# Idle products on TensorE ahead of three steps, each in the bank of the step that follows

## Chip, cores and metric

The kernel runs on one core of one Trainium2 chip. The metric is the device time of one execution in microseconds (us), as the median of several runs. The profile is of one further execution.

## The reference

Two layers on x of 4 sequences x 512 tokens x 256 features, in float32. What matters here:

```python
xn = layernorm(x)
x = x + L0_attn(xn) + L0_ffn(xn)     # elu feature maps, cumsum over tokens; top-32 of 512 genes
xn = layernorm(x)
x = x + L1_attn(xn) + L1_ffn(xn)

def L1_attn(x):
    q, k, v = split(rms(x) @ w_qkv.T)         # 256 each
    q, k = rms(q), rms(k)
    w = exp(k)
    y = sigmoid(q) * (cumsum(w * v) / (cumsum(w) + 1e-6))
    u, g = split(y @ w_swiglu.T)              # 1024 each
    return x + u * silu(g) @ w_out.T

def L1_ffn(x):                                # 16 experts, each token goes to 2
    y = sum over the two experts e of p_e * (swiglu(x @ w_gate_up[e]) @ w_down[e])
    return y + swiglu(x @ shared_gate_up) @ shared_down
```

## The kernel before

Each engine has its own order of steps, written out by hand as a list of calls in its block of the program. Engines meet only through semaphores. A step is a small function with the sequence b (0 to 3) and mostly a half or chunk, and on TensorE the PSUM bank that it writes: `dgate(0, 2, 5)` is the gate half of chunk 2 of sequence 0's gated products, into bank 5.

Ahead of about 340 us runs the front: for each sequence the first layer (turn1, logits, kproj, vproj, qproj, emturn, express, ffn, oproj), then the second layer's attention (turnr, turn2, qproj2, meanq, gates, kproj2, meank, vproj2) and the eleven chunks of dense gated products (dgate, dup, ddown). Behind it 47 tiles of 128 rows go through the routed experts (xturn, xup, hturn, xdown), mixed with the last sequence's chunks.

The eight banks are handed out by hand. `Banks.take` (and TensorE's `take`) waits until what last read the bank has given it back, and notes which semaphore and value will give it back next. Banks 6 and 7 accumulate ddown's products over a whole sequence. Banks 0 to 5 serve the other steps.

The steps around the change:

- `qproj2`, `kproj2`, `vproj2` (b, j): six products of 128x512 in fp32r each, from w_qkv1's high and low parts and FE, FF. They wait for rlow (DVE, L1006), the step's operands. The bank of qproj2 is given back by qhat (DVE, L1011), that of kproj2 by khat (L1018), that of vproj2 by wvtimes (L1023).
- `meanq` and `meank` (L395, L400): the mean of the squares as a float32 product. They wait for a fold on POOL, qfold (L1321) or kfold (L1325), which waits for the squares on ACT (L708). Behind meank: krms on ACT (L721, L723), then khat on DVE.
- `gates` (b): the router's logits, read by gatea (DVE) and so given back.
- `dgate`, `dup` (b, k): six products of 128x512 in fp32r each. All products made with the helper `products` have line 280.
- `awake(n)` (L292 for its product): n float32 products of a constant tile, 128x256, without a reader, into bank 6. It stands at eight places ahead of 73 us in the order.

In the order of TensorE the three places are: behind turnr(1, 0), turnr(1, 1) and ahead of dgate(0, 2); behind kproj2(1, 1) and ahead of meank(1); behind dup(1, 8) and ahead of kproj2(3, 0). The last step in the bank named by each new call: vproj2(0, 0) in bank 5, gates(1) in bank 2, qproj2(3, 0) in bank 5.

Of the kernel before, what the change touches and what calls it, by code (L numbers as in the profile page):

```python
# [83 lines left out]
def build(nc, x, vec, cst, wqkv0, wo0, wc, genes, wdu, wqkv1, wsg, wout, gate, sgu, sdn, gu, dn, part_d, out):  # L84
    with ExitStack() as ctx:
# [129 lines left out]
        banks = Banks([ctx.enter_context(nc.psum_tensor(f"bank{n}", [P, 512], F32)) for n in range(8)])  # L215
        bank_of = {}

        def ps(*key):
            return banks.t[bank_of[key]]
# [31 lines left out]
        def low_made(b, k):  # L251

            return s["rlp" if SPLIT[b] else "rl"], CHUNKS * sum(z == SPLIT[b] for z in SPLIT[:b]) + k + 1
# [11 lines left out]
        def chunk_of(k):  # L265

            if k < 3:
                return sgv, k * P, 352 + k * P, "sdn", min(P, 352 - k * P), k
            n = (k - 3) % 2 * P
            return [w[:, (k - 3) // 2] for w in wgv], D + n, n, "wout", P, k - 3  # L270
# [4 lines left out]
        def tensor(e):  # L275
            q = Queue(e)

            def products(o, terms):
                for n, (a, b) in enumerate(terms):
                    mm = e.matmul(o, a, b, start=n == 0, stop=n == len(terms) - 1)  # L280
                return mm

            def take(key, n, sem, value):
                bank_of[key] = n
                return banks.take(q, n, sem, value)

            def awake(n):

                q.wait_ge(s["wdr"], 1)
                o = banks.t[6]  # L290
                for _ in range(n):
                    e.matmul(o[:, 0:D].rearrange("p (k t) -> p k t", t=P), still[:, :], still[:, None, :].broadcast_to([P, 2, P]), start=True, stop=True)  # L292

            def turn1(b, h, n):
# [63 lines left out]
            def turnr(b, c, n):  # L358
                o = take(("tr", b, c), n, s["rlo"], 2 * b + c + 1)
                q.wait_ge(s["xr"], 4 * b + 4)  # L360
                for i in range(NT):
                    mm = e.transpose(o[:, i * P:(i + 1) * P], FDr[b % 2][:, i, c * P:(c + 1) * P], ident)
                mm.then_inc(s["tr"], 1)

            def turn2(b, c, n):
                o = take(("t2", b, c), n, s["x2"], 2 * b + c + 1)
                q.wait_ge(s["xn2"], 4 * b + 4)
                for i in range(NT):
                    mm = e.transpose(o[:, i * P:(i + 1) * P], FGw[b % 2][:, i, c * P:(c + 1) * P], ident)
                mm.then_inc(s["t2"], 1)  # L370

            def project2(b, j, n, first, sem, back, key):
                q.wait_ge(s["pl"], 1)
                o = take((key, b, j), n, back, 2 * b + j + 1)
                q.wait_ge(s["rlo"], 2 * b + 2)
                terms = []
                for c in range(2):
                    a, al = (w[:, c, (first + j) * P:(first + j + 1) * P] for w in qkv1)
                    h, l = FEr[b % 2][:, c, :], FFr[b % 2][:, c, :]
                    terms += [(a, h), (al, h), (a, l)]  # L380
                products(o[:, :], terms).then_inc(sem, 1)

            def qproj2(b, j, n):
                project2(b, j, n, 0, s["q2"], s["hq"], "q2")

            def kproj2(b, j, n):
                project2(b, j, n, 2, s["k2"], s["hk"], "k2")

            def vproj2(b, j, n):
                project2(b, j, n, 4, s["v3"], s["wv"], "v3")  # L390

            def meanq(b, n):
                o = take(("mq", b), n, s["rq"], 2 * b + 1)
                q.wait_ge(s["sqf"], b + 1)
                e.matmul(o[:, :], mean, FC[b % 2][:, 0, :], start=True, stop=True).then_inc(s["mq"], 1)  # L395

            def meank(b, n):
                o = take(("mk", b), n, s["rk"], 2 * b + 1)
                q.wait_ge(s["skf"], b + 1)
                e.matmul(o[:, :], mean, FC[b % 2][:, 0, :], start=True, stop=True).then_inc(s["mk"], 1)  # L400

            def gates(b, n):
                q.wait_ge(d["gate"], loaded["gate"])
                o = take(("gm", b), n, s["gt"], 7 * b + 2)
                q.wait_ge(s["x2"], 2 * b + 2)
                for i in range(NT):
                    mm = products(o[:, i * E:(i + 1) * E], [(FA[b % 2][:, c, i * P:(i + 1) * P], gtv[:, c, :]) for c in range(2)])
                mm.then_inc(s["gm"], 1)

            def hidden(b, k, n, first, sem, back, value, key):  # L410
                w, _, _, _, m, _ = chunk_of(k)
                h, l, made = (XH, HXr, s["xl"]) if k < 3 else (YH, HYr, s["yl"])
                q.wait_ge(s["pl"], HIDDEN[k])
                o = take((key, b, k), n, back, value)
                q.wait_ge(made, 2 * b + 2)
                terms = []
                for c in range(2):
                    a, al = (z[:, c, first:first + m] for z in w)
                    terms += [(a, h[:, c, :]), (al, h[:, c, :]), (a, l[:, c, :])]
                products(o[0:m, :], terms).then_inc(sem, 1)  # L420

            def dgate(b, k, n):
                back, value = (s["tg"], CHUNKS * b + k + 1) if DIRECT[b] else (s["g2"], CHUNKS * sum(not z for z in DIRECT[:b]) + k + 1)
                hidden(b, k, n, chunk_of(k)[1], s["dg"], back, value, "dg")

            def dup(b, k, n):
                hidden(b, k, n, chunk_of(k)[2], s["du"], s["dh"], CHUNKS * b + k + 1, "du")

            def ddown(b, k, n0, n1):
                _, _, _, name, m, r = chunk_of(k)  # L430
                oh, ol = pairs[name]
                if k == 0:
                    take(("acc", b, 0), n0, s["od"], 2 * b + 1)
                    take(("acc", b, 1), n1, s["od"], 2 * b + 2)
                c = CHUNKS * b + k
                q.wait_ge(s["pl"], DOWN[k])
                q.wait_ge(*low_made(b, k))
                for i in range(NT):
                    o = ps("acc", b, i // 2)[:, (i % 2) * D:(i % 2 + 1) * D]
                    h0, h1 = (h[0:m, 0, i * P:(i + 1) * P] for h in (HQ[c % 2], HSr[c % 2]))  # L440
                    for z, (a, w) in enumerate(((h0, oh), (h0, ol), (h1, oh))):
                        mm = e.matmul(o, a, w[0:m, r, :], start=k == 0 and i % 2 == 0 and z == 0, stop=False, skip_group_check=True)  # L442
                mm.then_inc(s["dw"], 1)
# [7 lines left out]
            def routed(g, *n):  # L451
                if g == 0:
                    take(("tab",), *n, s["rt"], 21)
                o = ps("tab")
                q.wait_ge(s["oh"], g + 1)

                for k in range(4):
                    mm = e.matmul(o[:, 0:3 * TW], r_bt[g % 2][:, k * P:(k + 1) * P], r_at[g % 2][:, 3 * TW * k:3 * TW * (k + 1)],
                                  start=g == 0 and k == 0, stop=False, skip_group_check=True)
                mm.then_inc(s["rtm"], 1)  # L460
# [54 lines left out]
            turnr(0, 1, 1); awake(2); emturn(1, 1, 5); turn2(0, 1, 1); qproj2(0, 0, 3); qproj2(0, 1, 5); qproj(1, 1, 0); emturn(1, 2, 1); express(1, 1)  # L515
            meanq(0, 2); gates(0, 0); emturn(1, 3, 1); express(1, 2); express(1, 3); kproj2(0, 0, 2); ffn(1, 0, 3); kproj2(0, 1, 1); ffn(1, 1, 5)
            ffn(1, 2, 0); dgate(0, 0, 4); ffn(1, 3, 3); dup(0, 0, 5); meank(0, 0); oproj(1, 0, 3); oproj(1, 1, 4); vproj2(0, 0, 5); vproj2(0, 1, 0)
            dgate(0, 1, 2); ddown(0, 0, 6, 7); dup(0, 1, 1); turnr(1, 0, 3); turnr(1, 1, 4); dgate(0, 2, 5); qproj2(1, 0, 3); qproj2(1, 1, 0)
            turn2(1, 0, 4); turn2(1, 1, 2); dup(0, 2, 1); meanq(1, 4); gates(1, 2); kproj2(1, 0, 5); kproj2(1, 1, 1); meank(1, 2); vproj2(1, 0, 4)
            ddown(0, 1, 6, 7); vproj2(1, 1, 3); dgate(0, 3, 0); turn1(2, 0, 2); dup(0, 3, 5); logits(2, 0, 1); ddown(0, 2, 6, 7); logits(2, 1, 4)  # L520
            turn1(2, 1, 3); dgate(0, 4, 2); kproj(2, 0, 3); logits(2, 2, 0); logits(2, 3, 1); dup(0, 4, 4); dgate(0, 5, 5); ddown(0, 3, 6, 7)
            emturn(2, 0, 3); dup(0, 5, 2); dgate(0, 6, 4); kproj(2, 1, 0); dup(0, 6, 5); express(2, 0, 3); ddown(0, 4, 6, 7); vproj(2, 0, 2)
# [9 lines left out]
            dup(1, 3, 4); ddown(1, 2, 6, 7); dgate(1, 4, 1); vproj2(2, 1, 2); dup(1, 4, 3); turn2(3, 0, 5); turn2(3, 1, 4); dgate(1, 5, 0)  # L532
            ddown(1, 3, 6, 7); gates(3, 1); dup(1, 5, 2); turnr(3, 0, 5); turnr(3, 1, 3); ddown(1, 4, 6, 7); dgate(1, 6, 4); dup(1, 6, 0); route1(1)
            dgate(1, 7, 2); qproj2(3, 0, 5); dup(1, 7, 4); qproj2(3, 1, 3); ddown(1, 5, 6, 7); ddown(1, 6, 6, 7); meanq(3, 0); dgate(1, 8, 0)
            dup(1, 8, 1); kproj2(3, 0, 5); kproj2(3, 1, 3); dgate(1, 9, 2); ddown(1, 7, 6, 7); dup(1, 9, 4); routed(0, 0); dgate(1, 10, 1)
            ddown(1, 8, 6, 7); dup(1, 10, 2); meank(3, 4); dgate(2, 0, 1); ddown(1, 9, 6, 7); routed(1); dup(2, 0, 2); vproj2(3, 0, 4); routed(2)
            dgate(2, 1, 1); ddown(1, 10, 6, 7); vproj2(3, 1, 5); dup(2, 1, 3); dgate(2, 2, 2); dup(2, 2, 4); ddown(2, 0, 6, 7); dgate(2, 3, 1)
            ddown(2, 1, 6, 7); dup(2, 3, 3); dgate(2, 4, 2); routed(3); ddown(2, 2, 6, 7); dup(2, 4, 4); dgate(2, 5, 1); dup(2, 5, 5); ddown(2, 3, 6, 7)
# [1034 lines left out]
```

## Time and profile before

| | us |
|---|---|
| median of 3 runs | 539.07 |
| lowest and highest | 535.23 and 539.32 |
| the profiled execution | 531.5 |
| its span | 529.7 |

The span is the time from the first to the last record of the profiled execution. The execution's own time has 1.8 us around it. It is shorter than all three other runs. Times in the rows are counted from the start of the span. PE is TensorE's products, PEld its weight loads. One float32 product of `awake` is two MATMUL records, and so is one of `meank`. The granted clock 1.00 is 2.4 GHz, 0.50 is 1.2 GHz.

### The profile page before, as it was taken

To read this page: it belongs to the slowest core of one execution; us is meant where nothing else is said; L and a number is where in the kernel's file an instruction comes from. 1 tells how busy PE (TensorE), PEld (TensorE's weight loads), DVE (VectorE), ACT (ScalarE), POOL (GpSimd) and SP (SyncE) were. 2 spreads that over 40 slices of the span, in tenths; PEclk is the share of its full clock that TensorE was granted. 3 is DMA by queue.
4 is the path that set the end of the run, shared out by engine and by line. 5 is a ranking of instruction groups with operands and counts; after the bars stand their busy time and mean duration, and the time that the engine had idled before them with its cause. 6 is when DMAs were issued, how large, how long until landed. Compare 5 with 4: busy or idle time off the path is not lost.

```text
span 529.7 us, 7444 instructions
## 1 busy us (share of the span) xinstructions
PE 507.5 (96%) x2488; PEld 384.8 (73%) x2488; DVE 354.0 (67%) x735; ACT 296.0 (56%) x577; POOL 272.7 (51%) x207
## 2 busy tenths in 40 slices
PE   7989999988999999999997999999999999999995
PEld 5565577766577766877885888887777777777684
DVE  4999995786998998847899895743232323323347
ACT  3788798785767758767653636225343343424321
POOL 0475648383472373383256346464576576666510
PEclk9999999998999999999999999999999999999999
DMA  8900031026020001037001850583322232223267
GB/s 271 372 6 1 1 124 37 0 100 220 1 80 40 1 1 41 1 129 243 1 1 44 292 179 14 187 232 98 108 91 89 71 100 83 97 80 89 71 242 265
DMA packets 19813, 54.32 MB, mean 103 GB/s; under 512 B 3312, under 2 KB 5792, under 8 KB 19776
## 3 DMA queue, kind: packets, MB, share of 16 engines
q1 hardware_dynamic: 15264, 41.52, 22.7%
q0 software_dynamic: 4512, 12.33, 7.7%
q8 instruction: 21, 0.34, 0.3%
q14 instruction: 16, 0.13, 0.1%
HBM read 36.14 MB, written 17.74 MB: 102 GB/s over the span
## 4 chain that ended last, share of the span: by engine, by line
PE 74%; DVE 15%; DMA 4%; issue 3%; ACT 2%; POOL 1%; SPq 1%; DVEq 0%; POOLq 0%; ACTq 0%
PE bank L280 52%; PE bank L442 9%; PE bank L355 3%; PE bank L474 2%; PE bank L501 2%; DMA fa<-in_x 2%; DMA ga<-y_rows 2%; DVE tk L972 1%; DVE m L970 1%; PE bank L328 1%; DVE fe L1029 1%; PE bank L400 1%; PE bank L292 1%; DVE tk L978 1%; DVE rw L1235 1%
## 5 line engine op out<-in xcount | busy, mean ns | idle before, releaser
L1214 DVE TENSOR_TENSOR m_h<-m_h,bank 128x176 f32<-128x176 f32 x47 | 15.8, 337 | 82.9 <-ACT m_h L789 82.9
L280 PE MATMUL bank<-mw,m_xt 128*128 x188 | 66.4, 476 | 0.2
L1362 POOL DMA_INDIRECT y_rows<-m_y,dest x47 | 46.9, 997 | 30.7 <-DVE m_y L1221 20.9
L1356 POOL DMA_INDIRECT xg<-xn_rows,tab x47 | 45.5, 969 | 28.0 <-PE bank L474 19.3
L280 PE MATMUL bank<-yhr,wsg_h 128*128 128x512 f32 x128 | 56.0, 437 | 0.8 <-ACT fc L721 0.8
L280 PE MATMUL bank<-hyr,wsg_h 128*128 128x512 f32 x128 | 50.1, 392 | 0.0
L280 PE MATMUL bank<-yhr,wsg_l 128*128 128x512 f32 x128 | 50.1, 391 | 0.0
L280 PE MATMUL bank<-mw,m_ht 88*128 x188 | 48.3, 379 | 0.0
L280 PE MATMUL bank<-fe,w_qkv 128*128 128x512 f32 x96 | 44.5, 594 | 0.6 <-ACT fe L622 0.6
L1347 POOL TENSOR_TENSOR hs0r<-hs,hq0r 128x512 fp32r<-128x512 f32 (+1 forms) x17 | 23.4, 1374 | 39.8 <-ACT hq0r L776 39.8
L280 PEld LDWEIGHTS bank<-mw,m_ht 88*128 88x128 f32 x188 | 35.2, 189 | 11.1 <-issue 0.4
L280 PEld LDWEIGHTS bank<-mw,m_xt 128*128 128x128 f32 x188 | 32.0, 189 | 14.9 <-issue 2.3
L789 ACT ACTIVATE m_h<-bank 128x176 f32<-128x176 f32 x47 | 14.9, 317 | 46.5 <-PE bank L280 46.5
L1098 DVE SCALAR_TENSOR_TENSOR hs<-hs,bank 128x512 f32<-128x512 f32 (+1 forms) x44 | 29.9, 680 | 14.7 <-PE bank L280 7.9
L1301 POOL TENSOR_TENSOR tk<-tk 128x512 f32<-128x512 f32 x16 | 21.3, 1334 | 27.9 <-ACT tk L680 27.8
L1347 POOL TENSOR_TENSOR hs1r<-hs,hq1r 128x512 fp32r<-128x512 f32 (+1 forms) x16 | 21.1, 1321 | 28.0 <-ACT hq1r L776 28.0
L782 ACT ACTIVATE m_xt<-bank 128x256 f32<-128x256 f32 x47 | 17.9, 381 | 29.9 <-PE bank L474 29.9
L572 ACT ACT_TABLE_LOAD x23 | 29.5, 1283 | 6.7 <-PE bank L442 5.6
L1088 DVE SCALAR_TENSOR_TENSOR hs<-hs,bank 128x512 f32<-128x512 f32 (+1 forms) x33 | 22.4, 680 | 15.4 <-ACT hs L771 15.4
L280 PEld LDWEIGHTS bank<-fe,w_qkv 128*128 128x128 f32 x96 | 17.5, 190 | 18.2 <-issue 16.3
L280 PE MATMUL bank<-w_wc,fe 128*128 128x512 f32 x64 | 29.9, 594 | 0.9 <-DVE w_wc L859 0.9
L280 PEld LDWEIGHTS bank<-yhr,wsg_h 128*128 128x128 f32 x128 | 24.1, 189 | 7.5 <-issue 1.7
(241 smaller groups left out, 1419.7 us busy)
## 6 DMA issues: line engine op xcount, KB each, us to landing
mw<-in_gu SPq DMA_DIRECT2D x16, 352.0 KB
ga<-y_rows SPq DMA_DIRECT2D x8, 512.0 KB, 8.1
mw<-in_dn SPq DMA_DIRECT2D x16, 176.0 KB
wsg_w<-in_wsg SPq DMA_DIRECT2D x4, 512.0 KB, 14.8
spilled_r<-fb SPq DMA_DIRECT2D x4, 512.0 KB, 2.8
spilled_x<-fa SPq DMA_DIRECT2D x4, 512.0 KB, 4.0
xn_rows<-fg SPq DMA_DIRECT2D x4, 512.0 KB, 3.6
hx<-spilled_x SPq DMA_DIRECT2D x4, 512.0 KB, 3.7
```

Source lines behind the costliest of these rows:

```text
L280: mm = e.matmul(o, a, b, start=n == 0, stop=n == len(terms) - 1)
L355: mm = e.matmul(o[:, i * D:(i + 1) * D], FF[b % 2][:, c, t:t + P], wov[:, c, :], start=False, stop=i + c == 2, skip_group_check=True)
L442: mm = e.matmul(o, a, w[0:m, r, :], start=k == 0 and i % 2 == 0 and z == 0, stop=False, skip_group_check=True)
L572: e.preload_act_table_set(name)
L782: e.activation(m_xt[j % 2][:, :], ps("jx", j)[:, 0:D], ACT.Copy).then_inc(s["jxc"], 1)
L1088: e.scalar_tensor_tensor(h, h, 1.0, ps("dg", b, k)[0:m, :], ALU.add, ALU.mult).then_inc(s["g2"], 1)
L1098: e.scalar_tensor_tensor(h[0:m, 1, :], h[0:m, 0, :], 1.0 if DIRECT[b] else 0.5, ps("du", b, k)[0:m, :], ALU.mult, ALU.mult).then_inc(s["dh ...
L1214: e.tensor_tensor(m_h[j % 3][:, :], m_h[j % 3][:, :], ps("ju", j)[:, 176:352], ALU.mult).then_inc(s["jh"], 1)
L1301: e.tensor_tensor(em, em, w, ALU.subtract).then_inc(s["tc"], 1)
L1347: e.tensor_tensor(HSr[c % 2][0:m, 0, :], HS[c % 2][0:m, 1, :], HQ[c % 2][0:m, 0, :].bitcast(F32), ALU.subtract).then_inc(s["rlp"], 1)
L1356: e.indirect_dma_start(out=xg[j % 3][:, :], out_offset=None, in_=xn_d, in_offset=bass.IndirectOffsetOnAxis(ap=tab[:, j:j + 1], axis=0)).th ...
L1362: e.indirect_dma_start(out=y_d, out_offset=bass.IndirectOffsetOnAxis(ap=dest[:, j:j + 1], axis=0), in_=m_y[j % 3][:, :], in_offset=None).t ...
```

## The change

`awake` takes the number of products and a bank, bank 6 if none is given. It waits until that bank has been given back, without taking it: the step behind it takes the bank as before. The eight calls from before stay in bank 6. There is one difference for them in principle, a wait on bank 6's giver, but they all stand ahead of the first step that takes bank 6, so there is nothing to wait for. Three calls are added. No other step moves, on any engine.

```diff
-            def awake(n):
+            def awake(k, n=6):
 
                 q.wait_ge(s["wdr"], 1)
-                o = banks.t[6]
-                for _ in range(n):
+                if banks.back[n]:
+                    q.wait_ge(*banks.back[n])
+                o = banks.t[n]
+                for _ in range(k):
                     e.matmul(o[:, 0:D].rearrange("p (k t) -> p k t", t=P), still[:, :], still[:, None, :].broadcast_to([P, 2, P]), start=True, stop=True)
...
-            ... turnr(1, 0, 3); turnr(1, 1, 4); dgate(0, 2, 5); ...
+            ... turnr(1, 0, 3); turnr(1, 1, 4); awake(3, 5); dgate(0, 2, 5); ...
-            ... kproj2(1, 0, 5); kproj2(1, 1, 1); meank(1, 2); ...
+            ... kproj2(1, 0, 5); kproj2(1, 1, 1); awake(6, 2); meank(1, 2); ...
-            dup(1, 8, 1); kproj2(3, 0, 5); kproj2(3, 1, 3); ...
+            dup(1, 8, 1); awake(8, 5); kproj2(3, 0, 5); kproj2(3, 1, 3); ...
```

## Rows read from the trace of the kernel before

**Rows 1.** The page: the span, and busy time by engine

```profile
span 529.7 us, 7444 instructions
...
PE 507.5 (96%) x2488; PEld 384.8 (73%) x2488; DVE 354.0 (67%) x735; ACT 296.0 (56%) x577; POOL 272.7 (51%) x207
```

**Rows 2.** TensorE's waits, 104 to 130 and 264 to 287: total, times, longest

```profile
PE bank L400 <- POOL fc L1325: 2.1, 1, 2.1
PE bank L280 <- DVE fc L1023: 1.1, 1, 1.1
PE bank L280 <- DVE ff1r L1006: 0.8, 1, 0.8
PE bank L395 <- POOL fc L1321: 0.7, 1, 0.7
...
PE bank L280 <- DVE fd L1011: 3.1, 1, 3.1
```

**Rows 3.** Busy time by stretch, with granted clock (PEclk), DMA share, GB/s

```profile
117.00:120.30 3.30, 3.30 (x11) 2.72 (x11) 2.63 (x17) 0.86 (x3) 3.23 (x3) 0.50 0.65 253
123.80:127.30 3.50, 3.35 (x6) 2.06 (x7) 1.01 (x6) 1.23 (x3) 0.01 (x1) 0.51 0.87 345
...
283.00:286.00 3.00, 0.00 (x0) 0.00 (x0) 2.97 (x5) 0.00 (x0) 2.35 (x2) 1.00 0.00 0
286.00:289.50 3.50, 3.45 (x15) 2.87 (x16) 3.47 (x5) 0.64 (x1) 0.84 (x1) 1.00 0.00 0
...
300.00:340.00 40.00, 40.00 (x230) 34.62 (x229) 29.08 (x43) 20.38 (x29) 20.55 (x14) 1.00 0.40 138
340.00:500.00 160.00, 159.79 (x792) 123.01 (x791) 54.15 (x123) 57.31 (x161) 97.80 (x98) 1.00 0.35 106
```

**Rows 4.** The chain that ended last: start, length, what

```profile
66.79 3.46 PE bank L292 x16
...
115.70 6.15 PE bank L280 x28
...
122.54 1.27 POOL fc L1325
...
123.95 2.06 PE bank L400 x2
...
126.04 0.70 ACT fc L721
...
127.52 1.29 DVE fg L1018 x2
...
141.48 8.17 PE bank L280 x24
...
285.32 0.69 DVE fd L1011
...
286.05 4.38 PE bank L280 x18
```

**Rows 5.** Line 292, 0 to 4 us: least/median/largest ns, first and last start

```profile
L292 PE MATMUL bank<-still x7: 634/634/796, 1.0 to 3.7; 128*128 128x256 f32 x7
```

**Rows 6.** Timeline of TensorE from 106 to 118 us: start, length, what

```profile
106.23 0.47 PE L280 MATMUL bank<-xhr,sgu_h 128*96 128x512 f32 x1 [1.07 <-DVE fc L1023]
...
107.47 0.40 PE L280 MATMUL bank<-hxr,sgu_h 128*96 128x512 f32 x1
108.62 0.47 PE L280 MATMUL bank<-fe1r,qkv_h 128*128 128x512 f32 x1 [0.76 <-DVE ff1r L1006]
...
115.53 2.07 PE L280 MATMUL bank<-w_gate,fa 128*128 128x16 f32 x16
```

**Rows 7.** Timeline of ACT and POOL around 112 us

```profile
111.65 0.60 ACT L708 ACTIVATE fc<-bank 128x512 f32<-128x512 f32 x1 [0.26 <-PE bank L280]
...
113.18 1.27 POOL L1321 TENSOR_TENSOR fc<-fc 128x512 f32<-128x512 f32 x1
```

**Rows 8.** Timeline of TensorE at 91 us, meank of sequence 0

```profile
91.66 1.02 PE L400 MATMUL bank<-fc,w_cst 128*128 128x512 f32 x2
```

More of the change, by code:

```diff
@@ L517, in tensor @@
             ffn(1, 2, 0); dgate(0, 0, 4); ffn(1, 3, 3); dup(0, 0, 5); meank(0, 0); oproj(1, 0, 3); oproj(1, 1, 4); vproj2(0, 0, 5); vproj2(0, 1, 0)
-            dgate(0, 1, 2); ddown(0, 0, 6, 7); dup(0, 1, 1); turnr(1, 0, 3); turnr(1, 1, 4); dgate(0, 2, 5); qproj2(1, 0, 3); qproj2(1, 1, 0)
-            turn2(1, 0, 4); turn2(1, 1, 2); dup(0, 2, 1); meanq(1, 4); gates(1, 2); kproj2(1, 0, 5); kproj2(1, 1, 1); meank(1, 2); vproj2(1, 0, 4)
+            dgate(0, 1, 2); ddown(0, 0, 6, 7); dup(0, 1, 1); turnr(1, 0, 3); turnr(1, 1, 4); awake(3, 5); dgate(0, 2, 5); qproj2(1, 0, 3); qproj2(1, 1, 0)
+            turn2(1, 0, 4); turn2(1, 1, 2); dup(0, 2, 1); meanq(1, 4); gates(1, 2); kproj2(1, 0, 5); kproj2(1, 1, 1); awake(6, 2); meank(1, 2); vproj2(1, 0, 4)
             ddown(0, 1, 6, 7); vproj2(1, 1, 3); dgate(0, 3, 0); turn1(2, 0, 2); dup(0, 3, 5); logits(2, 0, 1); ddown(0, 2, 6, 7); logits(2, 1, 4)
@@ L534, in tensor @@
             dgate(1, 7, 2); qproj2(3, 0, 5); dup(1, 7, 4); qproj2(3, 1, 3); ddown(1, 5, 6, 7); ddown(1, 6, 6, 7); meanq(3, 0); dgate(1, 8, 0)
-            dup(1, 8, 1); kproj2(3, 0, 5); kproj2(3, 1, 3); dgate(1, 9, 2); ddown(1, 7, 6, 7); dup(1, 9, 4); routed(0, 0); dgate(1, 10, 1)
+            dup(1, 8, 1); awake(8, 5); kproj2(3, 0, 5); kproj2(3, 1, 3); dgate(1, 9, 2); ddown(1, 7, 6, 7); dup(1, 9, 4); routed(0, 0); dgate(1, 10, 1)
             ddown(1, 8, 6, 7); dup(1, 10, 2); meank(3, 4); dgate(2, 0, 1); ddown(1, 9, 6, 7); routed(1); dup(2, 0, 2); vproj2(3, 0, 4); routed(2)
```

## Prediction

> **What bounds the kernel now.** I read the page's first lines, then TensorE's waits, then the chain of waits, then the granted clock by stretches, and last the timelines of the three places. TensorE is busy for 507.5 of the span of 529.7 us [rows 1], so what is worth anything must shorten or move its stream. The waits [rows 2] show where it stands: four waits between 104 and 130 us (1.1, 0.8, 0.7 and 2.1 us) and one of 3.1 us ahead of 287 us. Behind that there is next to none until the tail: between 300 and 340 us it is busy 40.00 of 40.00 us, and between 340 and 500 us 159.79 of 160.00 [rows 3]. The reader should take from this that a delay put into TensorE's stream after 286 us meets no pause that could swallow it, while one near 107 us does.
>
> The clock is the second thing. It is granted in full (2.4 GHz) nearly everywhere. Two stretches are at half (1.2 GHz): 117.0 to 120.3 us at 0.50 and 123.8 to 127.3 us at 0.51 [rows 3]. Ahead of the first TensorE had run sixteen records of only 16 columns [rows 6] and stood 0.7 us; ahead of the second it stood 2.1 us. But the 3.0 us from 283 to 286 us, wholly empty on TensorE, are followed by a clock of 1.00 [rows 3]. So a pause may bring the clock down, and in the profiled execution the longest one did not.
>
> **The change, part by part.** Three lines are added to TensorE's order. Each calls awake(k, n), which now first waits for bank n to come free and then issues k products of 256 columns. One call product is two MATMUL records: the existing awake(8) is 16 records in 3.46 us [rows 4], thus 0.216 us a record and 0.43 us a product. At half pace the trace has the first ones at the kernel's start, seven records that start from 1.0 to 3.7 us, 0.45 us each (2.7 / 6) [rows 5]. Nothing else is added, moved or removed on any engine, no DMA is touched, and no engine waits for an idle product. What is queued behind each wait is TensorE's own order only.
>
> The question at each place is whether TensorE stands on the operands or on the bank. The idle products wait for the bank too. Where the bank ends the pause, they cannot lie in it: they come after it, in front of real work.
>
> *Place A: awake(3, 5) ahead of dgate(0, 2).* Bank 5 last held vproj2(0, 0) and is freed by wvtimes(0, 0), which is line 1023. That is exactly the releaser of the 1.1 us wait [rows 2]. So the pause stays, and 3 x 0.43 = 1.3 us follow it. dgate(0, 2) then starts near 107.5 us in place of 106.23. Its last product starts at 107.47 and qproj2(1, 0) at 108.62, which waits for rlow (L1006) [rows 6]. Products of this kind follow each other at 0.25 us (five steps from 106.23 to 107.47), so qproj2 could have had TensorE at 107.72: 0.9 of the 1.3 us fall into that second pause, and 0.4 us remain. Behind it the squares of q run on ACT at 111.65 us, and the fold that follows on POOL starts at 113.18 us, held by the quotient ahead of it on POOL [rows 7]. The square then ends at 112.25 + 0.4 = 112.65, still 0.5 us before POOL takes the fold. TensorE's own next steps (turn2, dup) have the 0.7 us pause ahead of meanq (L395) as cover [rows 2]. Hence A costs 0. With the cover gone it costs 0.4, and with none of it 1.3. Below nothing it can only act by the clock: it leaves less of a pause ahead of 117.0 us. That is a rival below.
>
> *Place B: awake(6, 2) ahead of meank(1).* Bank 2 last held the gate logits, read by gatea(1) on DVE. They are off the way: the logits are done by 117.6 us (115.53 + 2.07 [rows 6]), gatea reads them at once, and kproj2(1, 1) ends at 121.85 [rows 4]. The pause ends with the fold on POOL (122.54 + 1.27 us, L1325), so the idle products do lie in it. Twelve records x 0.216 = 2.6 us from 121.7 us, where the last real product lets the next one in, end at 124.3 us. meank may start at 123.95 before [rows 4]: it is 0.35 us late. It then runs warm. In the trace it took 2.06 us at half clock [rows 4] and the same step of sequence 0 took 1.02 us [rows 8]. It ends at 124.3 + 1.02 = 125.3 in place of 126.01. The chain goes on from there through ACT at 126.04 and DVE at 127.52 (a wait of DVE for ACT) to TensorE at 141.48 us [rows 4], so B gives 0.7 us. If the clock stays high, vproj2 and its followers gain more on TensorE, but they aren't what ends that chain. If the clock would have been high anyway, B costs 0.35. Bounds: 1.3 gained (all of TensorE's own saving, 127.3 - 123.8 = 3.5 us at half clock being worth some 1.7, less 0.4) and 0.9 lost (rival 2). I take 0.7 gained.
>
> *Place C: awake(8, 5) ahead of kproj2(3, 0).* Bank 5 last held qproj2(3, 0) and is freed by qhat(3, 0), line 1011. That again is the releaser of the wait, 3.1 us [rows 2]: qhat ends at 285.32 + 0.69 = 286.01 and kproj2 starts at 286.05 [rows 4]. The operands of kproj2 had been ready since turnr and rlow, before qproj2 of the same sequence. So all eight products come behind the pause: 16 x 0.216 = 3.46 us. From 286.05 us the chain is on TensorE's stream [rows 4], and rows 3 show it full. The stages that feed it are fed by it, so they shift with it. A few places after 286 us where a step starts a tenth late may give 0.1 back. C costs 3.4 us. The lower end is 2.9 (some unseen slack of 0.5), the upper one is the half-pace price in a rival.
>
> The Trainium skill, "TensorE: Matmul & The Clock Gate", Part 1, says that the chip's default is the throttled clock and that activity releases it. It advises against idle gaps in the stream, which is what would speak for these products. By it, the longest pause should be the one that costs clock. The trace disagrees at C: a clock of 1.00 follows it [rows 3]. The rule's price there would be that of the second rival; by the row it is nothing.
>
> **The sum.** A 0, B -0.7, C +3.4: +2.7 us. Against the profiled execution (531.5 us, of which 529.7 are span and 1.8 lie around it) that is 534.2 us, and a span of 532.4. The median of the runs shown, 539.07, stands 7.6 us above that execution. The profile doesn't say why, so I add the difference to it: 541.8 us, or +0.5%.
>
> **The rivals.**
> 1. *The earlier slow stretch goes too.* A's products leave TensorE fuller ahead of 117.0 us. For it: the clock fell there with only small products and a pause of 0.7 us before. Against: the products lie ten microseconds earlier. Price: 3.3 us at half clock are worth 1.65 us, on the chain (L280, 6.15 us [rows 4]). Sum +1.0, 540.1 us. Chance 0.15.
> 2. *The clock falls on B's products.* About ten of their records are out by 123.8 us; the rest and meank run at half pace. meank starts near 124.8 and ends at 126.9, 0.9 late. Sum +0.9 + 3.4 = +4.3, 543.4 us. Chance 0.12.
> 3. *C's products run at half pace (the slower side).* It decides if the clock falls within the 3.1 us pause: 16 x 0.45 = 7.2 us instead of 3.46. Sum 7.2 - 0.7 = +6.5, 545.6 us, +1.2%. For it: a pause of 2.1 us was followed by the half clock. Against: rows 3 at 286. Also, a fall that lasts as long as the two seen (3.3 and 3.5 us) would slow only half of the products. Chance 0.08. By the skill's rule above this would be the likely one.
> 4. *C fills its pause after all*, as if bank 5 were free earlier: 3.46 - 3.1 = 0.4 late, less 0.7 from B: -0.3, 538.8 us. Against: the releaser's line and its end, 0.04 us before the start. Chance 0.06.
> 5. *More is won by the clock than the trace shows.* The unprofiled runs are 3.7 to 7.8 us above the profiled one. If these were slow stretches of 1.7 us each ahead of 130 us, the products could save several. Over 1% (5.4 us) needs five of them against C. Chance 0.05.
>
> **How the numbers follow.** The forecast has 0.54. It, rivals 1, 2 and 4 lie between 538.8 and 543.4 us. The three runs of before spread over 4.1 us, so the range takes some 1.3 us below and 2.1 above: 537.5 to 545.5. It leaves out rival 5, most of rival 3 and the outer scatter, together some 0.2. Faster by over 1% (about what a measurement can tell from no change) is rival 5: 0.05. Slower by over 1% is rival 3 and 0.02 of scatter: 0.10. Within 1%: 0.85.
>
> **What would show each step.** In the changed profile, the wait on L1023 of about 1.1 us must still be there, now ended by a record of L292, and the one on L1006 must be gone or 0.4 us. There must be no wait on POOL's L1325, or one under 0.3 us, and a clock near 1.00 from 121.7 to 127 us. The wait on L1011 must still be about 3 us, with 16 records of L292 over 3.46 us behind it and before kproj2. If the records of L292 lie inside that pause, C's step is wrong. If they take 0.43 us each, rival 3 holds. If meank ends no earlier against kproj2(1, 1)'s end than the 4.2 us of before (126.01 - 121.85), B's is wrong. The forecast fails above all if a measurable part of the 3.4 us comes back behind 286 us.

## The result, and the profile after

The changed kernel takes 540.95 us (median of 21 runs, 537.64 to 546.32), the kernel before 537.22 us (21 runs beside it, 533.59 to 543.27). The ratio is 1.0064, with a 95% interval of 1.0037 to 1.0092: 3.4 us slower (2.0 to 4.9), within the 1% of "no change" but clear of zero.

The page, span and busy time, where [rows 1] had 529.7 us and 507.5 (96%) with 2488 records:

```profile
span 540.4 us, 7511 instructions
...
PE 516.1 (95%) x2522; PEld 391.5 (72%) x2522; DVE 354.3 (66%) x735; ACT 296.1 (55%) x577; POOL 273.4 (51%) x207
```

The two profiled executions differ by 10.7 us, three times the difference of the medians. So the profiles have to be read place by place. TensorE's waits from 104 to 130, from 264 to 295 and from 350 to 510 us (total, times, longest), to be held against [rows 2]. Lines have moved by two: L294 is the idle product, L1025 is wvtimes, L1013 qhat, L1323 the fold ahead of meanq:

```profile
PE bank L294 <- DVE fc L1025: 1.1, 1, 1.1
PE bank L280 <- POOL hyr L1340: 0.5, 1, 0.5
PE bank L397 <- POOL fc L1323: 0.4, 1, 0.4
...
PE bank L294 <- DVE fd L1013: 3.1, 1, 3.1
PE bank L280 <- ACT fc L723: 0.8, 1, 0.8
...
PE bank L503 <- DVE m_h L1216: 3.3, 3, 2.0
PE bank L503 <- issue: 2.1, 2, 1.2
```

At the first and the third place the pause is as long as before, only its end is now an idle product. The waits on rlow and on meank's fold are gone. A wait of 0.5 us for POOL (L1340) is new: TensorE comes earlier to the step that needs it. In the routed stage TensorE waits 3.3 us for DVE and 2.1 us for nothing that the profile shows; the profile of before has no wait there from 350 to 510 us. TensorE's timeline at the three places:

```profile
106.48 1.56 PE L294 MATMUL bank<-still 128*128 128x256 f32 x6 [1.07 <-DVE fc L1025]
107.69 0.58 PE L280 MATMUL bank<-xhr,sgu_h 128*96 128x512 f32 x1
...
120.31 2.75 PE L294 MATMUL bank<-still 128*128 128x256 f32 x12
122.91 1.02 PE L402 MATMUL bank<-fc,w_cst 128*128 128x512 f32 x2
...
283.97 5.41 PE L294 MATMUL bank<-still 128*128 128x256 f32 x16 [3.06 <-DVE fd L1013]
289.03 0.58 PE L280 MATMUL bank<-fe1r,qkv_h 128*128 128x512 f32 x1
```

The eight products of the third place took 5.06 us (283.97 to 289.03), not 3.46. The windows (TensorE's busy time first, the granted clock third from the end) say why. They also show that both half-clock stretches of [rows 3] are gone, and that there is a new one in the routed stage:

```profile
117.00:120.30 3.30, 3.30 (x18) 2.80 (x18) 2.69 (x18) 1.85 (x4) 3.30 (x3) 1.00 0.70 271
123.80:127.30 3.50, 3.50 (x23) 3.12 (x22) 2.69 (x10) 3.27 (x8) 1.39 (x2) 1.00 0.77 302
...
285.80:288.60 2.80, 2.80 (x8) 2.26 (x7) 2.77 (x6) 0.91 (x2) 1.52 (x1) 0.50 0.29 114
...
340.00:500.00 160.00, 155.27 (x762) 119.39 (x761) 53.24 (x120) 54.87 (x153) 93.13 (x92) 0.99 0.35 107
...
438.80:442.30 3.50, 3.50 (x8) 2.33 (x8) 0.34 (x1) 0.32 (x1) 2.10 (x3) 0.53 0.33 102
```

The same marks in both profiles, in us from the start of the span, mostly the start of a step's first record on TensorE:

| | before | after | shift |
|---|---|---|---|
| meanq(1) | 114.60 | 114.82 | +0.2 |
| last product of kproj2(1, 1) | 121.44 | 120.08 | -1.4 |
| end of meank(1) | 126.00 | 123.93 | -2.1 |
| kproj(2, 0) | 141.48 | 139.39 | -2.1 |
| end of the pause ahead of kproj2(3, 0) | 286.05 | 283.97 | -2.1 |
| kproj2(3, 0) | 286.05 | 289.03 | +3.0 |
| hturn(0) | 363.24 | 366.27 | +3.0 |
| hturn(46) | 501.22 | 512.24 | +11.0 |

The front gains 2.1 us, of which 1.6 by the clock between meanq and kproj2 and 0.7 at meank, with 0.2 lost at the start. The third place costs 5.1. The last 8.0 us come in the routed stage, which the change does not touch: 5.4 are the two waits of L503 above, and some 1.7 (half of 3.4 us, an estimate) the half-clock stretch from 439.0 us. The experiments had to say which of these belong to the change.

### The profile page after: what moved, and what is told of

Read it like the earlier page. It is cut to its first block, busy times and chain, and to the rows that moved or that the text cites. A ratio compares the mean times of both kernels' runs of the same rounds, so it can differ in the third digit from the quotient of the medians.

```text
span 540.4 us, 7511 instructions
## 1 busy us (share of the span) xinstructions
PE 516.1 (95%) x2522; PEld 391.5 (72%) x2522; DVE 354.3 (66%) x735; ACT 296.1 (55%) x577; POOL 273.4 (51%) x207
## 4 chain that ended last, share of the span: by engine, by line
PE 76%; DVE 16%; issue 3%; ACT 2%; DMA 1%; POOL 1%; another core or an unknown queue 0%; SPq 0%; DVEq 0%; ACTq 0%
PE bank L280 52%; PE bank L444 10%; PE bank L357 3%; PE bank L294 2%; PE bank L503 2%; PE bank L476 2%; DVE tk L974 1%; DVE m L972 1%; PE bank L330 1%; DVE fe L1031 1%; DVE tk L960 1%; DMA w_vec<-in_vec 1%; DVE rw L1237 1%; DVE tk L980 1%; DVE m L956 1%
## 5 line engine op out<-in xcount | busy, mean ns | idle before, releaser
L280 PE MATMUL bank<-mw,m_xt 128*128 x188 | 67.5, 482 | 0.2 <-issue 0.2
L294 PE MATMUL bank<-still 128*128 128x256 f32 x104 | 28.5, 427 | 5.1 <-DVE fd L1013 3.1
```

## The experiments

Each kernel is compared with the kernel before on the same chip in the same rounds. The chips differ, so times are not to be compared across kernels, only ratios. Edits are shown against the kernel before, with the new `awake(k, n)` in it.

**Each place alone.** The first keeps only the third place:

```diff
-            dup(1, 8, 1); kproj2(3, 0, 5); kproj2(3, 1, 3); ...
+            dup(1, 8, 1); awake(8, 5); kproj2(3, 0, 5); kproj2(3, 1, 3); ...
```

> Only the eight idle products ahead of kproj2(3, 0), in bank 5; the other two places are as before. Theory (they lie behind the wait for bank 5 and push all that follows): 3.4 to 5.1 us more than before (+0.6 to +0.9%), the upper end where the clock falls while they run, as in the changed kernel's profile. In the profile: the wait of about 3.1 us still there, ended by the first idle product, 16 records behind it over 3.46 us or more. Rival (the changed kernel's difference comes from the later routed stage, whose stalls differ from run to run, and not from these products): within 0.3% of before, and no more than the kernel with the other two places.

Measured: 533.30 against 530.35 us, ratio 1.0057 (1.0032 to 1.0082), 3.0 us more. Its timeline has the step as predicted, at full clock, 3.37 us from the first product to kproj2:

```profile
283.79 3.72 PE L294 MATMUL bank<-still 128*128 128x256 f32 x16 [3.08 <-DVE fd L1013]
287.16 0.58 PE L280 MATMUL bank<-fe1r,qkv_h 128*128 128x512 f32 x1
```

The second has the other two places and not this one:

```diff
-            ... turnr(1, 1, 4); dgate(0, 2, 5); ...
+            ... turnr(1, 1, 4); awake(3, 5); dgate(0, 2, 5); ...
-            ... kproj2(1, 1, 1); meank(1, 2); ...
+            ... kproj2(1, 1, 1); awake(6, 2); meank(1, 2); ...
```

> The three and the six idle products of the two earlier places, none ahead of kproj2(3, 0). Theory: one or both stretches at half clock between 117 and 127 us go, so 0.7 to 2.3 us less than before (-0.1 to -0.4%) where the clock would have fallen, 0.4 more where it would not; the mean lies between -0.3% and 0. Rival (only the third place counts, the first two do nothing): equal to before. Rival (the third place does nothing): as slow as the changed kernel, +0.6%. In the profile: clock of 1.00 from 117 to 127 us.

Measured: 530.39 against 530.35 us, ratio 1.0003 (0.9979 to 1.0026). The third place alone carries the slowdown, and the rival that blamed the routed stage is out. But the front's gain doesn't show either: the interval reaches from -1.1 to +1.4 us, so a gain of a few tenths could be there. This kernel's profile is at full clock from 117 to 127 us and then falls behind the pause that still stands ahead of kproj2(3, 0):

```profile
283.60:286.80 3.20, 3.20 (x8) 2.52 (x9) 3.17 (x5) 0.63 (x1) 0.64 (x1) 0.50 0.00 0
```

The third has only `awake(3, 5)`, the fourth only `awake(6, 2)`.

> Only the three idle products ahead of dgate(0, 2). Theory of the prediction: no change (0 us, hidden by the pauses ahead of qproj2(1, 0) and meanq(1)); the stretch at half clock ahead of meank(1), behind the pause of 2.1 us, stays. Rival (A is what kept the clock up from 117 us in the changed kernel): 1.6 us less, -0.3%, and the profile shows 1.00 from 117 to 120 us.

Measured: ratio 1.0003 (0.9980 to 1.0025). A costs nothing that can be measured. Its profile still has the earlier half-clock stretch, so A doesn't prevent it, and the pause of 2.1 us ahead of meank with the later one:

```profile
117.60:120.90 3.30, 3.30 (x10) 2.58 (x9) 2.81 (x19) 0.85 (x2) 2.31 (x2) 0.53 0.72 223
```

> Only the six idle products ahead of meank(1). Theory: meank starts up to 0.4 us late and runs at full clock, 0.7 us less than before (-0.1%), with the stretch at half clock from 117 to 120 us still there in executions where it falls. Rival (the clock falls on the idle products): 0.9 us more (+0.2%).

Measured: ratio 1.0007 (0.9984 to 1.0030). The interval reaches from -0.8 to +1.6 us, so by itself it tells the forecast of -0.7 neither from nothing nor from the rival's +0.9. In the profile the clock didn't fall on the products.

**Doubling the third place**: `awake(16, 5)` there, nothing elsewhere.

> Sixteen idle products in place of eight ahead of kproj2(3, 0), in bank 5, and none at the other two places. Theory (nothing behind 286 us takes any of the delay back): 32 records x 0.216 = 6.9 us more than before (+1.3%), about twice the +0.57% of eight. Rival (some slack or some clock is won by the first products): the second eight cost more than the first, over 1.4% in all; rival (the delay is partly hidden behind other work): under 1.0%.

Measured: 543.04 against 535.51 us, ratio 1.0158 (1.0125 to 1.0192): 8.5 us (6.7 to 10.3). Eight cost 3.0 and sixteen 8.5. The forecast of 6.9 is just within the interval, but the measured 1.58% is where the first rival put it (over 1.4%, the second eight dearer than the first), and five runs do not tell the two apart. Only the second rival, under 1.0%, is out: no part of the delay is hidden. In the profile the sixteen take 8.5 us, since they hold a half-clock stretch as in the changed kernel:

```profile
283.26 8.86 PE L294 MATMUL bank<-still 128*128 128x256 f32 x32 [3.08 <-DVE fd L1013]
291.77 0.58 PE L280 MATMUL bank<-fe1r,qkv_h 128*128 128x512 f32 x1
```

**The same number of products, but inside the pause.** All six serving banks are held by DVE at that point. Bank 6 isn't, since it is TensorE's own running sum. A product with a zero moving operand can be added to it without a wait:

```diff
+            def within(k):
+                o = banks.t[6]
+                for _ in range(k):
+                    e.matmul(o[:, 0:D]..., still[:, :], w_cst[:, C_TRI:C_TRI + 1, None].broadcast_to([P, 2, P]), start=False, stop=False, ...)
-            dup(1, 8, 1); kproj2(3, 0, 5); ...
+            dup(1, 8, 1); within(8); kproj2(3, 0, 5); ...
```

> Eight idle products ahead of kproj2(3, 0) that need not wait for bank 5: they add zeros (a zero moving operand) to the running sum in bank 6, so the result is the same. None at the other two places. Theory (the cost of eight in bank 5 comes from lying behind the wait): they fill the pause of 3.1 us and end 0.4 us late; +0.4 us where the clock would not have fallen, and 1 to 2.4 us less than before where it would have, so between -0.4% and +0.1%. Rival (idle products cost their time wherever they stand, by what they do to the clock or the code): +0.6% as with bank 5.

Measured: ratio 1.0011 (0.9991 to 1.0031). The eight products are still there, and the 0.57% is not. They run from 282.56 us, just behind dup's last, and kproj2 comes in at its old time:

```profile
282.56 3.65 PE L300 MATMUL bank<-w_cst,still 128*128 128x256 f32 x16
285.85 0.58 PE L280 MATMUL bank<-fe1r,qkv_h 128*128 128x512 f32 x1
```

From kproj(2, 0), at 141.21 us here, it is 144.64 us to kproj2(3, 0), in the kernel before 144.57. The gain of 1 to 2.4 us that was expected where the clock would have fallen doesn't show. So the wait for the bank, and not the products, is what costs.

**How much cover the first place has**: `awake(8, 5)` ahead of dgate(0, 2) alone.

> Eight idle products in place of three ahead of dgate(0, 2), in bank 5; none at the other two places. Theory (0.9 us of the products lie in the pause ahead of qproj2(1, 0), and the fold on POOL waits 0.5 us longer than TensorE needs): 3.5 - 0.9 - 0.5 = 2.1 us more than before (+0.4%). Rival (place A is off the path altogether): equal to before. Rival (A's pauses cover nothing): +3.5 us, +0.65%.

Measured: 537.40 against 535.51 us, ratio 1.0041 (1.0018 to 1.0063), 2.2 us (1.0 to 3.4) where 2.1 was worked out. Both rivals are out, 3.5 us narrowly; to a tenth the size isn't measured. From bank 5 coming free to meanq it is 9.99 us in the profile, in the kernel before 8.37 us (106.23 to 114.60), so meanq is 1.6 us late and not 2.1. TensorE has no wait left up to the one ahead of meank, and meanq, put off by the products, now sets the chain:

```profile
105.70 3.72 PE L294 MATMUL bank<-still 128*128 128x256 f32 x16 [1.08 <-DVE fc L1025]
...
115.69 1.10 PE L397 MATMUL bank<-fc,w_cst 128*128 128x512 f32 x2
```

**Whether meank is on the path**: `awake(12, 2)` ahead of it alone.

> Twelve idle products in place of six ahead of meank(1), in bank 2; none at the other two places. Theory (the chain runs through meank, and the pause ahead of it is 2.1 us long): 24 records x 0.216 = 5.2 us, 3.1 of them behind the pause; less 0.3 to 0.7 for a meank at full clock: 2.4 to 2.8 us more than before (+0.5%). Rival (meank isn't on the way that sets the end, so that six products cost and gain nothing): under 0.2%.

Measured: 533.22 against 530.49 us, ratio 1.0045 (1.0028 to 1.0062), 2.4 us (1.5 to 3.3). meank starts 5.2 us behind the first idle product, and the chain that ends last runs through these products, so it has no slack for them. From the start of kproj2's last product to the end of meank it is 6.43 us, against a mean of 4.18 in the seven profiles without products there, 2.25 more:

```profile
119.33 5.34 PE L294 MATMUL bank<-still 128*128 128x256 f32 x24
124.51 1.02 PE L402 MATMUL bank<-fc,w_cst 128*128 128x512 f32 x2
```

**A version that fits both pauses.** `awake(5, 2)` ahead of meank(1), `within(7)` ahead of kproj2(3, 0), nothing at the first place. It ran on two chips, on the second beside `within(7)` alone.

> Five idle products ahead of meank(1) (2.2 us, as long as the pause) and seven ahead of kproj2(3, 0) that add zeros in bank 6 (3.0 us, as long as the pause); none at the first place. Theory: nothing is late at either place and the clock stays up: 1 to 3 us less than before (-0.2 to -0.5%). Rival (the clock's gain is too rare or too small to count): equal to before within 0.15%.

Measured on the first chip: ratio 0.9984 (0.9959 to 1.0008), not clear of zero. Its twelve runs lie between 532.88 and 538.32 us, nearly as wide as the 29 of the kernel before beside them (532.91 to 539.18). The profile is at full clock at both places, but the clock falls twice in the routed stage, each time at a wait of TensorE (1.5 us ahead of 402.4 us and 3.0 us ahead of 448.2 us):

```profile
403.00:406.50 3.50, 3.50 (x12) 2.62 (x11) 0.73 (x2) 1.38 (x5) 0.02 (x1) 0.51 0.00 0
447.40:450.90 3.50, 2.75 (x6) 1.74 (x7) 0.73 (x2) 1.16 (x4) 0.98 (x1) 0.51 0.15 52
```

> Only the seven idle products ahead of kproj2(3, 0) that add zeros in bank 6 (3.0 us, as long as the pause), none at the other two places. Theory: nothing is late, and where the clock would have fallen behind the pause (in four of eight profiles so far) 1.3 to 2.8 us are won: 0 to 1.4 us less than before on the mean (0 to -0.3%). Rival: equal to before within 0.1%.

(The expectation counts the clock's falls at the third place as four of eight; the traces up to then have five of eight.)

Measured: 529.03 against 530.49 us, ratio 0.9975 (0.9955 to 0.9994), as expected. Here the pause ahead of meank still stands, and the clock falls behind it:

```profile
122.00:124.70 2.70, 2.70 (x5) 1.48 (x6) 1.78 (x8) 0.84 (x2) 0.00 (x0) 0.50 0.99 344
```

> The kernel with five idle products ahead of meank(1) and seven zero-adding ones ahead of kproj2(3, 0), once more, to see whether it beats both kernels. Theory: -0.2 to -0.4%, and 0.1 to 0.2% less than the one with the seven alone. Rival: no difference from before that can be measured.

Measured: 528.06 against 530.49 us, ratio 0.9947 (0.9928 to 0.9966): 2.8 us faster than the kernel before. Its nine runs lie within 1.0 us (527.74 to 528.71), where the 26 of the kernel before beside them spread over 4.8. It gained more than the -0.2 to -0.4% expected. Against the seven products alone in the same rounds it is 1.0 us less (528.06 and 529.03), the 0.1 to 0.2% expected. No kernel has the five products ahead of meank(1) alone, so their share rests on this one difference. And the gain of 2.8 us was measured on this chip only: the same kernel gave 0.9984 on the other. The windows of its profile are full on TensorE, at full clock, at both places, and in the timeline nothing is late:

```profile
121.00:125.00 4.00, 4.00 (x21) 2.97 (x20) 2.46 (x10) 1.97 (x4) 0.62 (x1) 1.00 1.00 325
280.00:284.00 4.00, 3.99 (x19) 3.12 (x18) 3.97 (x6) 0.04 (x1) 2.40 (x2) 1.00 0.00 0
284.00:288.00 4.00, 4.00 (x21) 3.23 (x20) 3.93 (x7) 1.17 (x3) 1.54 (x1) 1.00 0.27 108
...
119.48 2.32 PE L294 MATMUL bank<-still 128*128 128x256 f32 x10
121.68 1.12 PE L408 MATMUL bank<-fc,w_cst 128*128 128x512 f32 x2
...
279.88 3.21 PE L300 MATMUL bank<-w_cst,still 128*128 128x256 f32 x14
283.11 0.50 PE L280 MATMUL bank<-fe1r,qkv_h 128*128 128x512 f32 x1
```

**The changed kernel with that one edit.** Against the changed kernel, `awake(8, 5)` becomes `within(7)`; the three and the six products stay.

> The changed kernel with one edit: the eight idle products ahead of kproj2(3, 0) are seven that add zeros in bank 6 without a wait for bank 5. The three and the six at the other two places stay. Theory (what makes the changed kernel slower is only that those eight wait for the bank): -0.2 to -0.5% against before, the six ahead of meank(1) costing up to 0.4 us that five did not. Rival (the other two places cost something too): 0 or more.

Measured: 534.86 against 535.57 us, ratio 0.9989 (0.9959 to 1.0018). The interval lies wholly below the changed kernel's (1.0037 to 1.0092), so the edit takes the slowdown away, though the two kernels ran in different rounds. It is not clear of zero, and -0.1% is short of the -0.2 to -0.5% expected. Whether the other two places keep something of the gain isn't settled by it.

## Why the prediction was right, point by point

**The time.** 541.8 was forecast and 540.95 measured. In differences: +2.7 forecast, +3.4 measured (2.0 to 4.9), so the 0.7 between them is within what the runs can tell. That the absolute times lie only 0.9 us apart is in part luck. The forecast stood on 539.07, the median of three runs; the 21 runs give 537.22. The base was 1.9 us too high and the difference 0.7 too low.

The 7.6 us between the profiled execution and the runs, which the prediction added without a reason, stay unexplained, but there is a hint. From hturn(0) to hturn(46) the profile of before takes 138.0 us, like the profiles on chips on which the kernel before takes some 530 us, and the changed profile 146.0 us, like those on chips on which it takes 535.5 (see the end of this section). That the two profiles come from different chips isn't shown.

**Place A, 0.** Right: ratio 1.0003 alone. In the profile dgate starts at 107.69 (forecast 107.5), the wait on rlow is gone, and the wait ahead of meanq is 0.4 instead of 0.7. That there is cover, and that it is limited, eight products showed: they cost 2.2 us (1.0 to 3.4), more than nothing and less than their own 3.5. Its size, 0.9 + 0.5 us by the prediction, is known less closely than 2.2 against 2.1 suggests: in that profile the eight products take 3.4 us up to the next step and meanq is 1.6 us late, which makes a cover of 1.8.

**Place C, +3.4.** Right, in place and size: +3.0 us alone (1.7 to 4.3). The argument was that the releaser of the pause is the giver of the bank, so the products come behind it. The same number of products without that wait gave +0.11% (-0.09 to +0.31%), not clear of zero. Rival 4, that they fill the pause, is out.

**Place B, -0.7.** The mechanism was right, and the size holds for a trace in which the clock would fall. From the start of kproj2's last product to the end of meank it is 4.56 us before and 3.85 after. But the term was taken from one execution. The clock fell behind this pause in five of the seven profiles without the products, and in none of the seven with them. Over the seven the stretch is 4.56, 4.42, 4.08, 3.61, 4.46, 3.61 and 4.55 us, mean 4.18. Six products make it 3.85, five 3.55. So six win 0.3 on the mean, and lose 0.2 where the clock stays up; five win 0.6. The term that was mis-sized is the 0.7 of "It then runs warm", taken as if meank always ran at half clock before. That is 0.4 us of the 0.7 between forecast and result, if the traces stand for the runs: the run with B alone (-0.8 to +1.6 us) can't confirm a gain of 0.3.

**Rival 1, the earlier stretch.** It was gone in the changed profile, and that was worth the 1.6 us (meanq to kproj2's last product: 6.84 us before, 5.26 after). But nothing shows that A did it. The stretch was missing in three of five profiles with products at A and in seven of nine without, and it was there in that of A alone. It changes from one execution to the next, so the 2.1 us that the front won between the two profiles are mostly not the change's.

**Rival 3, C at half pace.** It came in part: the clock fell 1.4 us after the pause (at 285.4 us), and the products took 5.06 us. The fall isn't a cost of the change, as the kernels without C show: from the end of the pause to hturn(0) it is 77.19 us before and 78.73, 79.97 and 78.48 in the profiles of the second to fourth experiment, in which the clock fell on the real products. With the pause left standing the clock fell in it or up to 1.4 us behind it in six of nine profiles, with products inside in none of five. The forecast read [rows 3] (a clock of 1.00 behind 286 us) as "nothing to win there". That was one of the three executions in nine in which it stays up, and it is the reading that failed. It didn't harm the sum: products behind the pause did not keep the clock up (it fell on them in two of the three kernels that have them). It hid the better version.

The verdict on the rule that the prediction weighed is thus reversed. "TensorE: Matmul & The Clock Gate", Part 1, of the Trainium skill has the throttle return when the engine is idle, and it holds in six of nine profiles at C, though not in the one that the prediction weighed it against. (The prediction calls the price by that rule that of the second rival; the rival that has the clock fall at C is the third.)

**What stays open.** The 8.0 us in the routed stage, and above all its waits. TensorE's wait there is for DVE, which waits for ACT, which stood for something that the profile doesn't show (2.5 us at 435 us). From hturn(0) to hturn(46) the kernels of the first four experiments, on one chip, take 137.5 to 138.6 us. On another chip, those with sixteen at the third place, with eight inside the pause, with eight at the first place and with both pauses filled take 143.1 to 148.0; the kernel before takes 530.35 us on the first and 535.51 on the second. On a third chip (before: 530.49) three kernels take 137.8 to 137.9, on a fourth (before: 535.57) one takes 142.6. So it goes with the chip, and not with the edit. Its cause wasn't tested.

## What to carry to other kernels

Before filling a pause, look at what ends it. If it is the bank (or buffer) that the filler must wait for as well, the filler becomes work behind the pause, at its full price. Put it where no wait is, here zeros added to an open sum, and make it no longer than the pause. And take a clock term from several profiles: one execution shows a fall or none, and a forecast of many runs needs the share of executions in which it falls.

## What the runs showed of the hardware

A pause of 2.1 us ahead of meank was followed by half clock in five of seven profiles, one of 3.1 us in six of nine, and kernels whose order is the same up to the pause go one way or the other (ahead of meank it fell in the kernel before, and not in the one with sixteen products at the third place). Most falls ahead of the tail lasted 3.4 us; in two of the six at the second of these places, with `awake(3, 5)` alone and with `awake(12, 2)` alone, the clock was at half for 6.8 us. Here is the latter (the window is 0.1 us longer than the fall):

```profile
284.50:291.40 6.90, 5.81 (x14) 4.57 (x15) 6.83 (x11) 1.75 (x3) 2.68 (x3) 0.51 0.29 118
```

The mean granted clock of a run goes with about half of the scatter between runs of one kernel. Over the 34 runs of the kernel before on the chip of the first experiments, a line through time against one minus clock has a slope of 268 us, meets full clock at 528.7 us and accounts for 0.51 of the variance; on the other three chips the slope is 269 to 321 us. If the whole run hung on TensorE's stream, a microsecond at half clock would cost half a microsecond and the slope would be the length of the run, 530 us. The slope of 268 means that it cost about a quarter (an estimate from the line). Not all half-clock time costs anything: with the third place alone, the clock is at half in the tail, where TensorE does nothing:

```profile
528.30:530.00 1.70, 0.00 (x0) 0.00 (x0) 0.00 (x0) 0.00 (x0) 0.00 (x0) 0.50 0.47 158
```

The kernel that fills both pauses had a mean clock of 0.999 in the nine runs on its second chip, the kernel before beside it 0.991. With that chip's slope of 269 us the difference of 0.008 is worth 2.1 us, most of the gain of 2.8 (an estimate). On the other of its two chips it had 0.997 against 0.994, and gained less (ratio 0.9984).
